# Attention tails of a four-layer megakernel: paired 32-column weighted values with their sums, and the clamp of one layer on VectorE

## The reference, cut to what matters

```python
scores = q @ k.T / 4                      # per head, 128 x 128
scores = clip(scores, -10000, 10000)      # L2 alone
out = softmax(scores) @ v                 # 128 x 16 per head
x = x + tanh(g) * (out.reshape(128, 256) @ Wo + bo)
```

## Time and profile before

| what | value |
|---|---|
| median of 3 runs | 2674.74 us (2673.25 to 2676.56) |
| the profiled execution | 2694.11 us |
| its span, first to last instruction | 2692.9 us |
| mean granted TensorE clock | 0.982 of full speed |
| PE busy | 2484.1 us |
| DVE busy | 1967.9 us |
| ACT busy | 1667.6 us |
| POOL busy | 1327.8 us |

### The profile page before, as it was taken

One profiled execution on the slowest core, in us unless ns is written; L12 is line 12 of the kernel. 1 busy time (PEld: TensorE's weight loads), 2 busy tenths in 40 slices (PEclk: granted clock), 3 DMA queues, 4 the chain that ended last, 5 costly groups with the idle time before them and its releaser, 6 DMA issues.

```text
span 2692.9 us, 66669 instructions
## 1 busy us (share of the span) xinstructions
PE 2484.1 (92%) x26500; PEld 2026.9 (75%) x26500; DVE 1967.9 (73%) x4666; ACT 1667.6 (62%) x4537; POOL 1327.8 (49%) x2117
## 2 busy tenths in 40 slices
PE   6899989898899999998899989999999989999999
PEld 4777767786677777777677777787777868788887
DVE  7778787869687786966565656667766676668998
ACT  4676767676567667765465555656566565666644
POOL 3232334242544434355664664545545464645777
PEclk9899999999899999999999999999999999999999
DMA  6000000000012221000111221100000000000010
GB/s 197 5 26 8 23 9 21 17 18 15 23 54 60 71 58 41 23 25 17 27 50 50 75 78 31 38 28 19 20 17 20 18 21 18 25 6 25 30 38 28
DMA packets 84191, 92.51 MB, mean 34 GB/s; under 512 B 15333, under 2 KB 77289, under 8 KB 83881
## 3 DMA queue, kind: packets, MB, share of 16 engines
q1 hardware_dynamic: 75432, 59.91, 7.2%
q0 software_dynamic: 8448, 28.34, 3.7%
HBM read 65.36 MB, written 22.85 MB: 33 GB/s over the span
## 4 chain that ended last, share of the span: by engine, by line
PE 48%; DVE 24%; POOL 13%; ACT 9%; issue 4%; DMA 2%; another core or an unknown queue 1%; SPq 0%; DVEq 0%; POOLq 0%; ACTq 0%
PE psum L376 12%; PE psum L369 8%; POOL big L1496 6%; PE psum L404 5%; PE psum L453 5%; DVE tiny L796 4%; PE psum L424 3%; PE psum L597 2%; PE psum L469 2%; ACT big L1310 2%; PE psum L383 2%; PE psum L397 2%; DVE big L815 2%; ACT big L1353 2%; PE psum L591 2%
## 5 line engine op out<-in xcount | busy, mean ns | idle before, releaser
L1310 ACT ACTIVATE big<-big 128x512 f32<-128x512 f32 x512 | 313.1, 630 | 211.3 <-DVE big L815 118.5
L796 DVE TENSOR_REDUCE tiny<-psum 128x8 f32<-128x1024 f32 x256 | 311.7, 1219 | 118.3 <-PE psum L453 112.1
L1471 POOL TENSOR_SCALAR tiny<-mv 128x1 f32<-128x1 f32 x224 | 56.9, 254 | 559.1 <-DVE mv L776 556.8
L424 PEld LDWEIGHTS psum<-ident,big 64*128 64x128 f32 x5120 | 208.6, 141 | 137.7 <-ACT big L1310 72.6
L424 PE MATMUL psum<-ident,big 64*128 64x64 f32 x5120 | 254.4, 232 | 62.2 <-ACT big L1310 41.5
L453 PE MATMUL psum<-head_keys,small 64*128 64x256 f32 x2048 | 286.0, 400 | 21.6 <-POOL head_keys L1488 8.0
L1488 POOL TENSOR_TENSOR head_keys<-big,head_rows 128x512 f32<-128x512 f32 x256 | 267.0, 1052 | 0.2
L815 DVE TENSOR_TENSOR big<-psum,tiny 128x512 f32<-128x512 f32 x384 | 251.3, 682 | 3.4
L1519 POOL TENSOR_TENSOR big<-big,tiny 128x512 f32<-128x512 f32 x128 | 135.1, 1061 | 233.6 <-DVE tiny L851 233.1
L1269 ACT ACTIVATE big<-psum 128x512 f32<-128x512 f32 x384 | 213.1, 600 | 59.7 <-PE psum L424 57.5
L1496 POOL TENSOR_SCALAR big<-big 128x512 f32<-128x512 f32 x128 | 190.8, 1503 | 115.2 <-DVE big L812 115.0
(11 more groups left out here) (340 smaller groups left out, 6638.1 us busy)
## 6 DMA issues: line engine op xcount, KB each, us to landing
ctxT<-in_ctxT SPq DMA_DIRECT2D x64, 128.0 KB, 2.2
after_L_xattn<-x SPq DMA_DIRECT2D x64, 128.0 KB, 1.7
mixture_out<-spare SPq DMA_DIRECT2D x46, 128.0 KB
x_in<-in_x SPq DMA_DIRECT2D x32, 128.0 KB
mixture_in<-xn SPq DMA_DIRECT2D x32, 128.0 KB, 1.7
x_in<-after_L_xattn SPq DMA_DIRECT2D x32, 128.0 KB
w_bits<-after_L_xattn SPq DMA_DIRECT2D x32, 128.0 KB, 2.2
spare<-in_L_w SPq DMA_DIRECT2D x2, 1024.0 KB, 6.4
```

Source lines behind the costliest of these rows:

```text
L424: last = pe.transpose(t.ab[:, half, at:at + P // 2], t.e[c][rows, j, :], m.ident[rows, rows])
L796: dve.tensor_reduce(top, s8, AX.X, ALU.max).then_inc(*t.dve.tell(p, f"{l}.top{r}"))
L1310: last = act.activation(flat, flat, ACT.Exp, scale=DH ** -0.5)
```

## The change

Four stages are put into a tuple `SUMMED`: L0, L2, self and L3, that is all narrow attentions.

- Values are laid out in pairs of heads: 48 columns per pair, 16 of the even head, 16 zeros, 16 of the odd head (`t.v_pairs`). Columns 0 to 31 are then the even head's stationary operand and columns 16 to 47 the odd head's, and the two accumulate into one 32-partition strip: the strip holds the two heads' outputs, features on partitions. POOL fills the zeros (128 per block in place of 16 ones); ACT's copy of the values writes into the two outer groups.
- The sums of the weights are made by a second set of the same matmuls with a constant operand `one_pair` (16 ones, 16 zeros, 16 ones), so every sum stands 16 times, in the same layout as the outputs. There are 32 matmul calls in place of 16.
- DVE takes the reciprocal of all sums (128x256, from PSUM) and multiplies the outputs (PSUM) with it, writing `t.oT`, which the output product reads. The copy of the bank, the four transposes, the two transposes and the last copy are gone.
- In L2, DVE clips the 128x1024 scores in PSUM in place before the maximum, and subtracts without a bound; the clip of the maxima and POOL's minima are gone, and ACT waits for DVE.
- The queries move to another part of `small`. All five strings of `ORDER` are written anew (PE's has 3368 turns instead of 3624, ACT's 2766 instead of 3022, POOL's 1244 instead of 1372; DVE's and SP's keep their length).

```diff
+SUMMED = ("L0", "L2", "self", "L3", )
...
     if l in SPREAD:
-        dve = dve.replace("top0", "top0 " + SPREAD[l] + "0").replace("top1", "top1 " + SPREAD[l] + "1")
+        dve = dve.replace("top0", SPREAD[l] + "0 top0").replace("top1", SPREAD[l] + "1 top1")
...
-        "pool": NORM["pool"] + " " + NARROW["pool"] + (" below0 below1 below2 below3" if cross == "L2" else "") + " xb",
+        "pool": NORM["pool"] + " " + NARROW["pool"] + " xb",
...
+for narrow in SUMMED:
+    STAGE[narrow]["pe"] = STAGE[narrow]["pe"].replace(" oP oT", "")
+    STAGE[narrow]["act"] = STAGE[narrow]["act"].replace(" oP oT", "")
...
     pe.wait_ge(*t.act.at(p, f"{l}.eT3"))
     pe.wait_ge(*t.pool.at(p, f"{l}.ones"))
+    if l in SUMMED:
+        for c in range(2 * KD):
+            for odd in range(2):
+                for j in range(CH):
+                    i = CH * (c % KD) + j
+                    h = 2 * i + odd
+                    pairs = m.one_pair[:] if c >= KD else t.v_pairs[:, i, :]
+                    last = pe.matmul(t.a[PAD * j:PAD * (j + 1), c * S:(c + 1) * S], pairs[:, odd * DH:odd * DH + PAD],
+                                     t.eTs[h // CH][:, h % CH, :], start=odd == 0, stop=odd == 1)
+        last.then_inc(*t.pe.tell(p, f"{l}.pv"))
+        yield
+        pe.wait_ge(*t.dve.at(p, f"{l}.o"))
+        tokens(pe, t.b, t.oT, m.w[l + "o"], D).then_inc(*t.pe.tell(p, f"{l}.out"))
+        yield
+        return
...
         dve.wait_ge(*t.pe.at(p, f"{l}.s{r}"))
+        if l == "L2":
+            flat = t.ab.rearrange("p r s -> p (r s)")
+            dve.tensor_scalar(flat, flat, CLAMP / DH ** -0.5, -CLAMP / DH ** -0.5, ALU.min, ALU.max
+                              ).then_inc(*t.dve.tell(p, f"{l}.clip{r}"))
+            yield
+            dve.wait_ge(*t.dve.at(p, f"{l}.clip{r}"))
...
-            if l == "L2":
-                dve.scalar_tensor_tensor(t.e[half], s8[:, mine, :], -CLAMP / DH ** -0.5, shift, ALU.max, ALU.subtract
-                                         ).then_inc(*t.dve.tell(p, f"{l}.e{2 * r + half}"))
...
+            dve.tensor_tensor(t.e[half], s8[:, mine, :],
+                              top[:, mine].rearrange("p (h o) -> p h o", o=1).to_broadcast([P, CH, S]), ALU.subtract
+                              ).then_inc(*t.dve.tell(p, f"{l}.e{2 * r + half}"))
+            yield
+    if l in SUMMED:
+        dve.wait_ge(*t.pe.at(p, f"{l}.pv"))
+        dve.reciprocal(t.o, t.a[:, D:2 * D]).then_inc(*t.dve.tell(p, f"{l}.den"))
+        yield
+        dve.wait_ge(*t.dve.at(p, f"{l}.den"))
+        dve.tensor_tensor(t.oT.rearrange("p k s -> p (k s)"), t.a[:, 0:D], t.o, ALU.mult
+                          ).then_inc(*t.dve.tell(p, f"{l}.o"))
+        yield
+        return
...
+    if l in SUMMED:
+        pairs = t.v_pairs.rearrange("p i (g d) -> p i g d", g=3)
+        return act.activation(pairs[:, :, 0:3:2, :], bank[:, 0:D].rearrange("p (i g d) -> p i g d", i=H // 2, g=2), ACT.Copy)
...
-                if l == "L2":
-                    act.wait_ge(*t.pool.at(p, f"{l}.below{c}"))
-                else:
-                    act.wait_ge(*t.dve.at(p, f"{l}.e{c}"))
+                act.wait_ge(*t.dve.at(p, f"{l}.e{c}"))
...
+    if l in SUMMED:
+        return
     act.wait_ge(*t.pe.at(p, f"{l}.pv"))
     act.activation(t.oP, t.a, ACT.Copy).then_inc(*t.act.tell(p, f"{l}.oP"))
...
+    if l in SUMMED:
+        pool.memset(t.v_pairs[:, :, DH:2 * DH], 0.0).then_inc(*t.pool.tell(p, f"{l}.ones"))
...
-    if l == "L2":
-        for c in range(4):
-            e = t.e[c % 2].rearrange("p h s -> p (h s)")
-            pool.wait_ge(*t.dve.at(p, f"{l}.e{c}"))
-            pool.tensor_scalar(e, e, 0.0, None, ALU.min).then_inc(*t.pool.tell(p, f"{l}.below{c}"))
-            yield
...
+    pool.memset(m.one_pair[:, 0:DH], 1.0)
+    pool.memset(m.one_pair[:, DH:2 * DH], 0.0)
+    pool.memset(m.one_pair[:, 2 * DH:3 * DH], 1.0)
...
-    t.qT = small[:, D + 32:2 * D + 32].rearrange("p (k s) -> p k s", s=S)
+    t.v_pairs = small[:, 0:H // 2 * 3 * DH].rearrange("p (i c) -> p i c", i=H // 2)
+    t.qT = small[:, 2 * D + 32:3 * D + 32].rearrange("p (k s) -> p k s", s=S)
```

More of the change, by code:

```diff
@@ new lines @@
+        "0100311010212033133211121002101232230231131313133223012010022221223312312133331033310122310200311322"
+        "3123203010220323233211313123002020000000233201321030310300321010212221100133033011012112111002101221"
+        "0202303223033103122332130011022220331212121323313330130322102311220031032002110231233002120230300110"
+        "1102200233033223200332101301013312230202010111300201133233100111210112100210232320230311322121212232"
+        "3312321221130300023213321223130333011231202032311031233202303010212132301131132023203002303202001031"
@@ new lines @@
+        "020311221302211021321320303033022302033228732873002380073873a8007a798330a9837a897807933a893097a08300"
+        "8a097a07c8b9ba89ca00087900b8ac7b8cbac890bc7980780a8b7cab87b9ca98bca8007aca7b0798ba97a9c00a8a9bc07ba7"
+        "09abc89b856c69b58b97ac867c6cabc596b595b6a5cba6c57656ca565b9c96b7856ca5879bc6b698758c956ac6a6956bc5ab"
+        "cacb567c59b69576a956597578a68c65bc59b7967c6c5ba5b6ac86c75896596b575ab8cac685a9656a56b75b98768ac695cb"
+        "795cb6786abcb578a675768a89b7c65b6b5798b5ac95689c6c5a6b565975c9b6c565"
@@ L295 @@
+        "2302303013011232122210303030123013110212220031103220131232031020203031133132212003213313300012111120"
+        "223022030760367763339896798678708789966ab77096a79a8b60b00087a679bba8697976a88a9b79ba67986798baa45b65"
+        "49b5a4a889b6679b45547aa85b45498ba85549b5ba4a4b567856874a994a5bb544688659475b5b6448a79a6975b85448a96b"
+        "54ba594a775658645ba89b4a479676a55a8448bb5544"
     ),
     "sp": (
[L297 removed]
@@ L301 @@
+        "20940031101221230313040123020121320304241312203340301142042312302010412412334403018729378ba8cb98aab7"
+        "c9065bc5b56aa9866c777a598965c58cba769bc65"
     ),
@@ L798, in dve_heads @@
         dve.wait_ge(*t.dve.at(p, f"{l}.top{r}"))
-        if l == "L2":
-            dve.tensor_scalar(top, top, CLAMP / DH ** -0.5, -CLAMP / DH ** -0.5, ALU.min, ALU.max
-                              ).then_inc(*t.dve.tell(p, f"{l}.clip{r}"))
-            yield
-            dve.wait_ge(*t.dve.at(p, f"{l}.clip{r}"))
         if l in BIASED:
@@ L809, in dve_heads @@
             mine = slice(CH * half, CH * (half + 1))
-            shift = top[:, mine].rearrange("p (h o) -> p h o", o=1).to_broadcast([P, CH, S])
-            if l == "L2":
-                dve.scalar_tensor_tensor(t.e[half], s8[:, mine, :], -CLAMP / DH ** -0.5, shift, ALU.max, ALU.subtract
-                                         ).then_inc(*t.dve.tell(p, f"{l}.e{2 * r + half}"))
-            else:
-                dve.tensor_tensor(t.e[half], s8[:, mine, :], shift, ALU.subtract
-                                  ).then_inc(*t.dve.tell(p, f"{l}.e{2 * r + half}"))
-            yield
+            dve.tensor_tensor(t.e[half], s8[:, mine, :],
+                              top[:, mine].rearrange("p (h o) -> p h o", o=1).to_broadcast([P, CH, S]), ALU.subtract
+                              ).then_inc(*t.dve.tell(p, f"{l}.e{2 * r + half}"))
+            yield
+    if l in SUMMED:
[7 more added lines that the diff above has]
+        return
     got = t.b.rearrange("p (h d) -> p h d", h=H)
@@ L1276, in act_heads @@
         yield
-        act_values(act, t, t.b if l == "self" else t.a).then_inc(*t.act.tell(p, f"{l}.v"))
+        act_values(act, t, t.b if l == "self" else t.a, l).then_inc(*t.act.tell(p, f"{l}.v"))
         yield
@@ L1292, in act_heads @@
         act.wait_ge(*t.pe.at(p, "self.v"))
-        act_values(act, t, t.b if l == "self" else t.a).then_inc(*t.act.tell(p, "self.v"))
+        act_values(act, t, t.b if l == "self" else t.a, l).then_inc(*t.act.tell(p, "self.v"))
         yield
@@ L1483, in pool_heads @@
     pool.wait_ge(*t.act.at(p, f"{l}.k"))
-    if l == "L0" and p == 0:
+    if l == "none" and p == 0:
         pool.memset(t.v_rows[:, H * (DH + 1):H * (DH + 2)], 0.0)
-    pool.memset(v[:, :, DH:DH + 1], 1.0).then_inc(*t.pool.tell(p, f"{l}.ones"))
+    if l in SUMMED:
+        pool.memset(t.v_pairs[:, :, DH:2 * DH], 0.0).then_inc(*t.pool.tell(p, f"{l}.ones"))
+    else:
+        pool.memset(v[:, :, DH:DH + 1], 1.0).then_inc(*t.pool.tell(p, f"{l}.ones"))
     for r in range(2):
```

235 lines of the change are left out of this document (105 added, 130 removed).

## The result

The changed kernel takes 2744.32 us, the median of three runs (2741.86 to 2752.18), against 2674.74 before: a ratio of 1.0268, 95% interval 1.0253 to 1.0282, **69.6 us slower**. The forecast, 2700 us and slower, had the side; its growth of 25 us is little more than a third of the real one. The profiled execution took 2741.86 us (span 2740.6). That of the kernel before was 0.7% above its median, so between the two profiles the growth shows as 47.7 us only.

What follows compares the result with a forecast made beforehand. The prediction took PE, about 92% busy in both stages, as the bound. Its terms, +23 us for PE, -14 for the clamp's detour and +16 for DVE load, gave +25: 2700 us against the 2674.7 median, range 2622 to 2765.

Steps and rivals of the forecast that it cites:

- What more DVE load costs: Both stages: 249 us more DVE work slows the kernel by 16 us, 6 in the second stage, 10 in the first.
- PE's +23: Attention tail on PE: +118 us of weighted-value pieces less 95 us of transposes, net +23 us, at most +37.
- The other half of the step: First stage: 42 us more DVE work, priced at DVE's 24% share of the chain, costs 10 us.
- the step's path: Other lanes' maxima and subtractions queue on DVE behind the wide reciprocal, 1.7 us at a time; PE's transposes wait for them.
- The sign that it set for a bound on DVE: PE's idle time in the second stage growing by more than 40 us would show DVE as the bound.
- The premise behind it: Both stages: PE, at 92.3% and 92.8%, is close to its bound whatever its neighbours do.
- The weighted values, the transposes and the durations: Attention tail: 64 pieces at 28.75 ns, +118 us; transposes gone, -95 us; reciprocal 1.7 us, clip 1.22 us.
- The clamp's term: L2: dropping POOL's detour saves PE 14 us, at most 34, while DVE gains 63 us of work.
- Order: All five rewritten lists: no row prices them, taken as zero, some 13 us either way.
- The first: Tail's division: the reciprocal runs near the plain rate, 0.42 us, giving 2674 us, no change; chance 0.14.
- The second: L2: the chain through POOL's clamp, not PE's occupancy, sets the time; -54 us, 2621 us; chance 0.35.
- The third: Both stages: DVE becomes the bound at a 79% queue ceiling, +27 and +53 us, 2755 us; chance 0.16.

Runs made afterwards that it cites:

- tail with a short reciprocal: Kernel before with the paired tail, its lists less the dropped turns, clamp still on POOL, reciprocal over 16 of 256 columns: 2711.62 us, ratio 1.0136.
- the short reciprocal: Changed kernel with the reciprocal taken over 16 of the 256 columns only: 2627.33 us, ratio 0.9818.
- the clamp alone: Kernel before with L2's scores clipped on DVE in PSUM, POOL's minima and their turns removed, tail unchanged: 2659.40 us, ratio 0.9936.
- the unread reciprocal: Kernel before plus a 256-wide DVE reciprocal of ones behind each block's product, its result read by nobody: 2779.19 us, ratio 1.0404.
- the order of before: Changed kernel with the five order lists of the kernel before, less the turns that no longer exist: 2772.18 us, ratio 1.0368.

## Why the prediction was right in its side and wrong in its size

The four kernels between before and after make one way from the one to the other, and its steps stand against the terms of the sum:

```
step                                        predicted   measured
tail with a short reciprocal                      +23        +37   2675.04 -> 2711.62
the reciprocal made long       within the +16 of DVE        +77   2711.62 -> 2788.87
clamp to DVE                    -14, and its part of the 16  -17   2788.87 -> 2772.18
lists rewritten                                     0        -28   2772.18 -> 2744.32
sum                                               +25        +69
```

By another way the steps would be shared out otherwise (the reciprocal 117 at the end of it); in both of these orders the reciprocal is the largest.

**The step that failed is "What more DVE load costs".** It priced 249 us of DVE at 16. The runs put 0.30 to 0.61 us on each microsecond, with 0.40 to 0.61 for the reciprocal's 192 alone, where the term has 0.06. The side that came out right hangs on this term too, and not on PE's +23: with the short reciprocal the changed kernel is 48 us faster than before, where the sum without DVE's term is +9. The step reasoned that the first stage has DVE at 79% and the second at 65% beside almost the same PE share, so DVE's load hardly matters to PE. The two stages do different work, and PE's share is no measure of what a stage would gain or lose: the changed kernel's second window has PE at 92.4%, the faster one with the short reciprocal at 97.0%, and before 92.8%. The other half of the step, 24% of the chain as the price of the first stage's 42 us, was the better instrument, though below every price measured on DVE: 0.24 on all 249 us would have given 60 us and a sum of +69, the right number by luck, since the gain of the lists was left out as well.

Nor did the step's path hold. It had PE's transposes of the other lanes wait behind the reciprocal; the direct row is 10.7 us, the one by way of ACT's exponentials shrank, and the longest is the block's own output product with 44.5. The sign that it set for a bound on DVE, 40 us more of PE's idle time in the second stage, did not show either: it went from 84 us to 88 in a window of the same length.

**The premise behind it was wrong too.** "PE is close to its bound in both stages whatever its neighbours do" would make 118 us of pieces cost 118; they cost 70 in the kernel before, 32 and 3 in the changed one. PE's pieces follow each other without a gap in a dense microsecond, but its busy time is no measure of its work: the same instructions took 2468 us beside the short reciprocal and 2502 beside the long one.

**The weighted values, the transposes and the durations were right.** The pieces kept their pace, the tail with the short reciprocal has 18 us more of PE's busy time than before (2502.5 us against 2484.1) where the net was +23, the reciprocal came out at 1.75 us between bounds of 0.42 and 4.0, and DVE at 81% of the span, POOL at 42%, ACT at 57%, as forecast. The reading of the reciprocal from the 16-element row, with the plain slope taken off, gave 6.1 ns an element; (1749 - 251) / 240 is 6.2. The Trainium skill, VectorE: DVE Perf Modes, section "First, the fixed hardware budget", has it as an iterative divide with a repeat count of 8. The trace agrees in kind, with 1749 ns for 256 elements where a plain copy takes 420; the estimate of 2.1 us that was worked out from the repeat count is 0.35 us too high.

**The clamp's term was right in sign and near in size**: -14 with a few microseconds of DVE against it, -16 alone. PE's wait that it was priced from, 33.6 us in the second stage, is 10.2 in the changed kernel:

```profile
PE psum L421 <- ACT big L1328: 10.2, 15, 1.9
```

Before its exponentials in the changed kernel ACT still idles 212.8 us, 210.1 of it for DVE, where POOL had 91 us of it before: with the tail beside it, POOL's place was taken by DVE's queue.

**Order** was priced at zero with 13 us either way; it is 28 beside this tail, and by the sum above more beside the short reciprocal. No row of before could show it, and the term's bounds were too narrow.

**The rivals.** The first fell with the reciprocal's duration. The second, faster by the shorter L2 chain, is what the clamp alone does, 16 us of its 54; beside the tail the clamp still gives 17, and the tail's 114 (37 + 77) drown it. The third named the place, long instructions at the head of a queue that four lanes share, and its 2755 us is the nearest number of all, 11 us off. Its law, a ceiling of 79% for an ordered queue, is not what the runs show: the changed kernel's first window has DVE at 82.1% (895.22 of 1090), and in the kernel before the unread reciprocal cost 106 us with the second window's DVE at 73.2% (849.13 of 1160). The price is there below the ceiling as well. Its 0.16 was too little, and the forecast's 0.35 went to a case that took DVE for nearly free.

What stays open: why the price of the same reciprocal is 0.40 with before's lists and the clamp on POOL, and 0.61 with the new lists and the clip on DVE, and which of the two makes the difference; and why a microsecond of the clip costs half of one of the reciprocal. No run separates these.

## What to carry to other kernels

An engine at 92% need not be the bound, nor one at 73% free: when lanes share ordered queues, an instruction on a second engine can cost a good part of itself, here 0.30 to 0.61 of it, even when nobody reads its result. Price such a change before making it by adding unread work of the same length to the kernel that exists, on each engine in turn, and take those two slopes rather than the busy shares. Here they would have given, as an estimate, 0.60 x 23 + 0.48 x 249 - 14 = +119 us, against the +97 measured in the order of before (2772.18 - 2675.68): a quarter too high, where the forecast's +25 was a quarter of it. Trading six transposes and two copies for more weighted values and one wide reciprocal on a shared queue was a bad trade here; taking a clamp off a detour through a third engine was a good one, even at 61 us more of DVE.

## What the runs showed that was not expected

- The granted clock fell where PE was given less to do: 0.961 over the span without the sums and with the long reciprocal, 0.979 with them. Of the 118 us of sum pieces that were taken out, PE's busy time lost 58; by the estimate above the clock accounts for some 45 of the missing 60.
- A reciprocal takes 1742 ns on 256 elements read from SBUF and 1749 from PSUM: the source hardly matters to it, the number of elements does (249 ns for 16 from PSUM).
- PE's busy time for the same 29828 instructions differs by 33 us between two kernels that differ in one DVE instruction.
